# Second cross attention of an eight-layer kernel: another home for the query weight, other places for its splits, value products in alternating order

## The reference

```python
x = x + _L0_xattn_ref(_layernorm(x), ctx, ...)      # first cross attention
x = x + _L0_ffn_ref(_layernorm(x), ...)             # first feed-forward, 28 experts
x = x + _L1_xattn_ref(_layernorm(x), ctx, mask, Wq, Wk, Wv, Wo, q_norm_w, k_norm_w)
x = x + _L1_ffn_ref(_layernorm(x), ...)             # second feed-forward
...                                                 # four more layers

def _L1_xattn_ref(hidden_states, cross_attention_states, attention_mask, Wq, Wk, Wv, Wo, q_norm_w, k_norm_w):
    H, KVH, HD = (32, 8, 128)
    q = (hidden_states @ Wq.T)...   # 32 query heads of 128
    k = (cross_attention_states @ Wk.T)...   # 8 key heads
    v = (cross_attention_states @ Wv.T)...   # 8 value heads
    q = _rmsnorm(q, q_norm_w)
    k = _rmsnorm(jnp.repeat(k, GROUPS, axis=1), k_norm_w)
    scores = q @ k.T / sqrt(HD) + attention_mask
    probs = softmax(scores)
    return (probs @ v)... @ Wo.T
```

## Time and profile before

| | |
|---|---|
| time, median of 3 runs | 1603.42 us (1601.63 to 1606.4) |
| the profiled execution | 1602.04 us, its span 1600.3 us |
| TensorE busy | 1512.0 us, 94% of the span |
| VectorE busy | 1054.3 us, 66% |
| ScalarE busy | 815.2 us, 51% |
| GpSimd busy | 358.2 us, 22% |
| DMA | 60.23 MB, mean 38 GB/s |
| second cross attention, first to last query product | 690.3 to 1298.9 us of the span |

### The profile page before, as it was taken

How to read it: one execution, slowest core, us unless ns; L and a number is a source line. 1 busy time by engine, 2 the same in 40 slices (tenths; PEclk the granted TensorE clock), 3 DMA queues, 4 the chain that set the end, 5 groups by cost and what they waited for, 6 DMA issues and landing times.

```text
span 1600.3 us, 27791 instructions
## 1 busy us (share of the span) xinstructions
PE 1512.0 (94%) x9626; PEld 1324.2 (83%) x9626; DVE 1054.3 (66%) x2557; ACT 815.2 (51%) x2862; POOL 358.2 (22%) x370
## 2 busy tenths in 40 slices
PE   6999999999999999979999999999999998789996
PEld 5999999999999987868888888888888877667775
DVE  6566556655665568766666666666666677787775
ACT  4456455544554554345655555555555542454542
POOL 4102010210111021122313132222222221543420
PEclk9999999999999999989999999999999999898998
DMA  5100100100001000010101010101100001111001
GB/s 201 38 27 27 41 27 27 67 27 28 28 27 40 27 26 27 27 40 28 40 28 42 25 67 1 67 15 52 41 27 31 5 8 53 44 54 33 21 14 56
DMA packets 14193, 60.23 MB, mean 38 GB/s; under 512 B 2036, under 2 KB 3444, under 8 KB 8936
## 3 DMA queue, kind: packets, MB, share of 16 engines
q1 hardware_dynamic: 14056, 58.46, 10.2%
HBM read 56.36 MB, written 2.10 MB: 37 GB/s over the span
## 4 chain that ended last, share of the span: by engine, by line
PE 52%; issue 29%; DVE 11%; POOL 4%; ACT 3%; DMA 0%; POOLq 0%; DVEq 0%; SPq 0%; ACTq 0%
PE psY L843 12%; PE psQ L768 8%; PE psKV L788 8%; PE psSO L831 2%; PE psSO L737 2%; PE psQ L753 2%; PE psTP L753 1%; POOL wo L474 1%; PE psTP L798 1%; PE psSO L738 1%; PE psTP L816 1%; PE psQ L699 1%; PE psSO L712 1%; PE psKV L712 1%; PE psQ L1108 1%
## 5 line engine op out<-in xcount | busy, mean ns | idle before, releaser
L843 PE MATMUL psY<-wo,oT 128*128 128x512 f32 x1536 | 386.3, 400 | 1.8 <-DVE oT L1669 1.3
L843 PEld LDWEIGHTS psY<-wo,oT 128*128 128x128 f32 x1536 | 279.6, 189 | 66.3 <-POOL wo L474 2.2
L768 PE MATMUL psQ<-wq,hT 128*128 128x512 f32 x768 | 212.3, 414 | 0.1
L474 POOL TENSOR_TENSOR wo<-stage_o,wo 128x512 fp32r<-128x512 f32 (+2 forms) x71 | 91.7, 1320 | 322.3 <-ACT wo L1239 322.3
L575 POOL TENSOR_TENSOR rms<-ms_eps,minus_half 128x5 f32<-128x5 f32 x64 | 74.7, 1167 | 390.1 <-DVE ms_eps L1832 390.1
L768 PEld LDWEIGHTS psQ<-wq,hT 128*128 128x128 f32 x768 | 137.5, 192 | 25.0 <-DVE wq L1669 1.5
L1308 ACT ACTIVATE prob<-s_sb,neg_mx 128x64 f32<-128x64 f32 x256 | 86.1, 337 | 110.4 <-DVE neg_mx L1819 110.4
L1311 ACT ACTIVATE prob<-wide,neg_mx 128x128 f32<-128x128 f32 x256 | 99.7, 391 | 74.5 <-DVE neg_mx L1819 74.3
L1239 ACT ACTIVATE pT<-psTP 128x512 fp32r<-128x512 f32 (+1 forms) x128 | 62.3, 487 | 131.9 <-PE psTP L816 131.9
L788 PEld LDWEIGHTS psKV<-wkv,arena 128*128 128x128 f32 x768 | 99.6, 190 | 18.6 <-DVE kT L1669 14.3
L1669 DVE TENSOR_TENSOR pT<-psTP,pT 128x512 fp32r<-128x512 f32 (+1 forms) x128 | 70.6, 551 | 65.9 <-ACT pT L1239 65.1
(11 more groups left out here) (287 smaller groups left out, 3243.5 us busy)
## 6 DMA issues: line engine op xcount, KB each, us to landing
stage_q<-in_wq SPq DMA_DIRECT2D x16, 1024.0 KB, 5.2
stage_o<-in_wo SPq DMA_DIRECT2D x16, 1024.0 KB, 4.8
stage_kv<-in_wkv SPq DMA_DIRECT2D x12, 512.0 KB, 3.6
stage_q<-in_ctx SPq DMA_DIRECT2D x16, 256.0 KB, 2.8
stage_o<-in_ctxT SPq DMA_DIRECT2D x2, 1024.0 KB, 6.6
stage_q<-in_base SPq DMA_DIRECT2D x2, 1024.0 KB, 5.0
out<-x_res SPq DMA_DIRECT2D x8, 256.0 KB, 2.3
x_res<-in_x SPq DMA_DIRECT2D x1, 1536.0 KB, 12.4
```

The source lines that it names most:

```text
L474: g.tensor_tensor(dst[LO], stage, dst[HI].bitcast(f32), ALU.subtract).then_inc(ld[what + "_lo"], 1)
L768: m = mm(psQ[:], lat(xl, k, n), wq[:, wl, k, :], start=k == 0 and i == 0, stop=k == KT - 1 and i == 2)
L843: m = mm(psY[:], oT[:, ol, h, :], wo[:, wl, h, :], start=h == 0 and i == 0, stop=h == HQ - 1 and i == 2)
```

## The change

1. `attend` of the second attention goes over the passes outside and the batches inside, so its six products alternate between partitions 0 to 63 and 64 to 127.
2. The query weight gets two homes. Loads with an odd number from 9 on go to part 0 of `hT`, even ones to `wq` (`wq1_in_context`, `wq_slice`); the moving operand is there read in eight runs of 64 columns (`by_eight`). So the next group's weight is split while the present one is used: a quarter in each of steps 3, 4, 5 and 6 of a group (`high_wq1` on ScalarE, `low_wq1` on GpSimd). GpSimd now makes all four low parts, VectorE none.
3. In steps 2 to 7 of a group GpSimd waits for `prob` of the step before (the normalised probabilities) ahead of its weight splits, of the output, key and value weights too.
4. Load 9, the first group's, is split in the first feed-forward (steps 4 to 7 on ScalarE, after norms 2 to 5 on GpSimd), and the key and value weight before the last two norms.
5. `k_scale` is gone: `kT_hi` scales while it copies, and `kT_lo` is one instruction that scales and subtracts, both from the PSUM bank.
6. At the passage to the attention the first query product comes ahead of the transposes of the norm of tile 6, which move from the feed-forward into the first `kv_proj`.

```diff
@@ -358,6 +358,15 @@
         return psS[:, 2 * P:3 * P] if n < 4 else psP[:, 0:P]
+    def wq1_in_context(load):
+        return load >= 9 and load % 2 == 1
+    def wq_slice(load, hl, k):
+        return hT[:, hl, k, :, 0] if wq1_in_context(load) else wq[:, hl, k].rearrange("p (n t) -> p n t", n=NT)
+    def by_eight(ap):
+        return ap.rearrange("p (n t) -> p n t", n=NT)
@@ -468,10 +477,10 @@
-        def low(what, dst, stage, hi_count):
+        def low(what, dst, stage, hi_count, done=None):
...
             pool.wait_ge(ld[what + "_hi"], hi_count)
-            g.tensor_tensor(dst[LO], stage, dst[HI].bitcast(f32), ALU.subtract).then_inc(ld[what + "_lo"], 1)
+            g.tensor_tensor(dst[LO], stage, dst[HI].bitcast(f32), ALU.subtract).then_inc(ld[done or what + "_lo"], 1)
@@ -517,6 +526,10 @@
                 low("wo", halves(wo, k), stage_o[:, k], count + k + 1)
+        def low_wq1(load, k):
+            low("wq", (wq_slice(load, HI, k), wq_slice(load, LO, k)), by_eight(stage_q[:, k]), load * 4 + k + 1,
+                "wq_lo" if k < 2 else "wq_lo_v")
@@ -562,8 +575,9 @@
             ln_rstd(2, n)
-            if n == 6:
-                low_wq(9)
+            if 2 <= n < 6:
+                low_wq1(9, n - 2)
+            if n == 5:
@@ -574,8 +588,11 @@
                                 ALU.pow).then_inc(s["rms"], 1)
+            if t.exists and t.res(8) in (2, 3, 4, 5, 6, 7):
+                pool.wait_ge(s["prob"], t.back(1).c + 1)
+            if 3 <= t.res(8) < 7 and t.exists:
+                low_wq1(t.div(8) + 10, t.res(8) - 3)
             if t.res(8) == 7 and t.exists:
-                low_wq(t.div(8) + 10)
@@ -709,7 +726,8 @@
                 for i, (xl, wl) in enumerate(PASSES):
-                    m = mm(ring3(t)[:], lat(xl, k, t), wq[:, wl, k, :], start=k == 0 and i == 0, stop=False)
+                    m = mm(by_eight(ring3(t)[:]), lat(xl, k, t), wq_slice(WQ_DENSE[f.index], wl, k),
+                           start=k == 0 and i == 0, stop=False)
@@ -765,13 +783,15 @@
                     for i, (xl, wl) in enumerate(PASSES):
-                        m = mm(psQ[:], lat(xl, k, n), wq[:, wl, k, :],
+                        m = mm(by_eight(psQ[:]), lat(xl, k, n), wq_slice(st.div(NT) + a.wq0, wl, k),
...
                     pe.wait_ge(setup["ctxT"], 8)
+                    pe.wait_ge(FS["x_add"], NT)
+                    ln_transpose(2, NT - 2, lambda: pe.wait_ge(LNS[2]["lo"], ln_at(2, NT - 2)))
@@ -820,15 +840,17 @@
                 n = u.res(NT)
-                for b in range(2):
+                if a.index == 0:
+                    for b in range(2):
+                        for i, (vl, pl) in enumerate(PASSES):
+                            m = mm(psO0[:, b * 256:(b + 1) * 256], a.v[:, n, vl, b * HD:(b + 1) * HD],
+                                   pT[:, pl, b * 256:(b + 1) * 256], start=i == 0, stop=i == 2)
+                else:
                     for i, (vl, pl) in enumerate(PASSES):
-                        if a.index == 0:
-                            lhsT, rhs = a.v[:, n, vl, b * HD:(b + 1) * HD], pT[:, pl, b * 256:(b + 1) * 256]
-                        else:
+                        for b in range(2):
                             rows = slice(b * S, (b + 1) * S)
-                            lhsT, rhs = a.v[rows, u.res(a.ring), vl, 0:HD], pT[rows, pl, 0:256]
-                        out = psO0[:, b * 256:(b + 1) * 256] if a.index == 0 else psO[:, b, 0:256]
-                        m = mm(out, lhsT, rhs, start=i == 0, stop=i == 2)
+                            m = mm(psO[:, b, 0:256], a.v[rows, u.res(a.ring), vl, 0:HD], pT[rows, pl, 0:256],
+                                   start=i == 0, stop=i == 2)
@@ -952,7 +974,7 @@
                 hidden_transpose(f, u)
-            if 0 <= v < NT - (f.index == 0) and next_ln != 4:
+            if 0 <= v < NT - 2 * (f.index == 0) and next_ln != 4:
@@ -1251,6 +1273,9 @@
+        def high_wq1(load, k):
+            high("wq", wq_slice(load, HI, k), by_eight(stage_q[:, k]), (load + 1) * 16)
@@ -1286,11 +1311,13 @@
-                if a.rms:
-                    act.wait_ge(s["wq_used"], st.t * 4 + 4)
-                else:
-                    act.wait_ge(s["q_units"], st.t + 2)
-                high_wq(st.div(8) + (10 if a.rms else 1))
+                act.wait_ge(s["q_units"], st.t + 2)
+                high_wq(st.div(8) + 1)
+            def next_wq1(st):
+                need(act, s["wq_used"], st.div(8) * 32)
+                high_wq1(st.div(8) + 10, st.res(8) - 3)
@@ -1326,11 +1353,11 @@
                 act.wait_ge(s["k_tr"], a.kv_n(st) + 1)
-                src = k_sb[:, HD:2 * HD] if a.rms else psKV[:, 0:2 * keys]
                 if a.rms:
-                    act.wait_ge(s["k_scaled"], st.t + 1)
-                copy(a.kT[:, st.res(a.ring), HI], src).then_inc(s["kT_hi"], 1)
+                    nc.scalar.activation(a.kT[:, st.res(a.ring), HI], psKV[:, 0:HD], ACT.Identity,
+                                         scale=wqk[:, 2:3]).then_inc(s["kT_hi"], 1)
+                    return
+                copy(a.kT[:, st.res(a.ring), HI], psKV[:, 0:2 * keys]).then_inc(s["kT_hi"], 1)
@@ -1380,7 +1407,9 @@
                     unit_hi(k)
-                if t.exists and not early and t.res(8) == (7 if a.rms else 6):
+                if t.exists and a.rms and 3 <= t.res(8) < 7:
+                    next_wq1(t)
+                if t.exists and not a.rms and not early and t.res(8) == 6:
@@ -1463,11 +1492,12 @@
                      hT[:, hl, k, :, 0:4:3, :].bitcast(f32)).then_inc(setup["ctxT"], 1)
-            if t == 8:
+            if 4 <= t < 8:
+                act.wait_ge(setup["ctxT"], t + 1)
+                high_wq1(9, t - 4)
+            if t == 7:
...
                 high_wkv(5)
-                act.wait_ge(FS["dense"], NT)
-                high_wq(9)
@@ -1842,11 +1872,6 @@
-            def k_scale(st):
-                dve.wait_ge(s["k_tr"], a.kv_n(st) + 1)
-                V.tensor_scalar(k_sb[:, HD:2 * HD], psKV[:, 0:HD], wqk[:, 2:3], None, ALU.mult).then_inc(s["k_scaled"], 1)
@@ -1857,8 +1882,12 @@
                 dve.wait_ge(s["kT_hi"], a.kv_n(st) + 1)
-                src = k_sb[:, HD:2 * HD] if a.rms else psKV[:, 0:2 * keys]
-                sub_hi(a.kT[:, st.res(a.ring), LO], src, a.kT[:, st.res(a.ring), HI]).then_inc(s["kT_lo"], 1)
+                if a.rms:
+                    V.scalar_tensor_tensor(a.kT[:, st.res(a.ring), LO], psKV[:, 0:HD], wqk[:, 2:3],
+                                           a.kT[:, st.res(a.ring), HI].bitcast(f32), ALU.mult,
+                                           ALU.subtract).then_inc(s["kT_lo"], 1)
+                    return
+                sub_hi(a.kT[:, st.res(a.ring), LO], psKV[:, 0:2 * keys], a.kT[:, st.res(a.ring), HI]).then_inc(s["kT_lo"], 1)
@@ -1926,8 +1955,8 @@
                     qk_normalise(t)
-                if t.exists and t.res(8) == (7 if a.rms else 6):
-                    low_wq(t.div(8) + (10 if a.rms else 1))
+                if t.exists and not a.rms and t.res(8) == 6:
+                    low_wq(t.div(8) + 1)
@@ -1935,8 +1964,6 @@
                 if a.kv_new(t):
-                    if a.rms:
-                        k_scale(t)
@@ -2015,8 +2042,6 @@
                 ln_lo(f.ln, NT - 1)
-            if f.index == 0 and t == NT + 2:
-                low_wq(9)
```

## The result

The changed kernel takes 1586.44 us (median of 4 runs, 1586.05 to 1588.07) where the kernel before, beside it, took 1602.94: a ratio of 0.9896, 95% interval 0.9878 to 0.9913. That is 16.5 us, against 20.2 forecast as a difference and 1583 as a time. Timed again on another chip it took 1586.08 against 1604.54, a ratio of 0.9884 (0.9866 to 0.9901), 18.5 us. The profiled execution took 1586.25 us, its span 1584.4.

The account below looks back on a forecast made before the run. TensorE was taken as the bound, busy 579.99 of 593 us. The terms 9.9 + 4.2 + 4.1 + 2.0 = 20.2 us came off the profiled 1602.04, giving 1581.8, or 1583 us as a median; range 1576 to 1590, 8-in-10 range 1574 to 1595.

Parts of the forecast that it names:

- a group's step 0 above 9.8: Sign of being wrong: the first step of a group of eight still taking over 9.8 us, where it took 10.64.
- the waits for `kT`: Sign of being right: TensorE's weight loads wait under 2 us in all for `kT`, where they waited 14.3.
- The key product of step 0: Sign of being right at the passage from the feed-forward: this product starts at about 691 us instead of 695.29.
- Query weight in two homes: Steps 7 and 0 of each group: 1.42 us of excess goes, seven times, 9.9 us; ends 6.4 and 9.9.
- lower end of 6.4: Query weight's gain if half of the wait for `kT` stayed, 0.5 us in each group, 3.5 in all.
- I take the whole excess: Steps 7 and 0: all of 0.08 + 1.34 = 1.42 us over a plain step vanishes, seven times, 9.9 us.
- `k_scale`: Behind step 2, `kT`'s low part reads PSUM and ends earlier: 0.6 us, seven times, 4.2; ends 0 and 5.3.
- The passage: From feed-forward to attention: query product first, its weight split early; 4.1 us, with 2.2 below and 5.5 above.
- The end: Step 63: TensorE's waits of 1.27 for `prob` and 0.76 for `oT` both go, 2.0 us, between 0 and 3.
- Value products and strided weight: Reordering the six value products and reading the query weight in eight runs of 64 columns: 0 each.
- the rival of 15 us: Value products do gain, as the old order ran one after the other but for one pair: 15.4 us more, 1568; chance 0.06.
- The rival of half found again elsewhere: Stalls return in the feed-forward (4.4), step 7 (3.5) and step 2 (4.2), leaving 8.1 us: 1595; chance 0.17.

Follow-up runs that it names:

- x1: The kernel before with only the order of the value products changed, by pass and then by row half: 1605.49 us, 1.0007 of the kernel before.
- x4: The changed kernel with step 0's key and value products waiting for each half of their weight where read: 1579.55 us (0.9854), the second time 1583.57 (0.9874).
- x5: The changed kernel without GpSimd's waits for `prob` in steps 2 to 7: 1587.81 us, 0.9899 of the kernel before.
- x3: The changed kernel with VectorE's scaled key copy put back and both parts of `kT` made from it in SBUF: 1592.83 us, 0.9927 of the kernel before.
- x6: The changed kernel with the transposes of tile 6's norm back in the feed-forward, ahead of the first query product: 1588.52 us, 0.9901 of the kernel before.
- x9: The changed kernel with the scaled key copy and the old place of tile 6's transposes both put back: 1592.57 us, 0.9937 of the kernel before.

## Why the prediction was right, and where its terms were not

The bound, TensorE, the sign and the range were right. The time came out 3.4 us above the forecast. Of the signs that the prediction named, `neg_mx` (0.17 us throughout), the value products, the weight read in runs and `prob` came as said. But "a group's step 0 above 9.8", one of its signs of being wrong, came too, at 10.02, and the waits for `kT` are 2.4 us, not under 2. The key product of step 0 starts at 693.95, not at about 691, but TensorE stood 3.3 us later already when the feed-forward began. By its terms:

**Query weight in two homes: 9.9 forecast, 5.1 measured**, below even my lower end of 6.4: 0.06 in step 7 and 10.65 - 10.02 = 0.63 in step 0, seven times, and 0.2 more in one step 7 that took 9.59 before (9.60 in `x1`). The step that failed is "I take the whole excess". The prediction had GpSimd's 2.75 us for the key and value weight "beside it", because the list named only `kT`. That split was late too, by 0.14 us less, and became the wait. `x4` shows it, as taking that wait alone away brings step 0 to 9.30, 5.1 us in all. GpSimd's waits behind `prob` are worth about 2 us of the gain (`x5`).

**`k_scale`: 4.2 forecast, 6.75 measured by undoing it.** Behind step 2, 0.57 against 0.6: right, and for the reason given, as `x3` has the low part at 1.04 us and the changed kernel at 0.35. What I left out is steps 60 to 62, where the norm's transposes wait for the low part of `pT`, which stands behind `kT` on VectorE (1.05 us), 0.8 at the end, and 0.05 in each step 0.

**The passage: 4.1 forecast, 4.7 up to the key product.** The size is right by a wrong working. I put the 5.16 us of the first query product down to the clock; its last three products had to wait for VectorE's split, which ended at 694.44, and `x1` shows the waits, 0.85 and 0.73 us, at full clock. And 2.9 of the 4.7 come from splitting early (`x6`), not from the order. Up to the query transposes 4.5 are left, as 4.78 follow where 4.61 did: the 0.2 that I had put down. What follows to step 8 varies with the clock: 71.2 and 72.7 us in the two profiles of the changed kernel.

**The end: 2.0 forecast, 2.4 measured** (36.11 against 33.72 from step 63's start to the feed-forward's transposes, both without half clock). The profile of before has 37.33 there, with a stretch of half clock in it. `prob` went; `oT` keeps 0.71 of 0.76, so the working was off there too. Of the 2.4, 0.8 belong to `k_scale` (`x3`) and 1.6 to the query weight (`x9`).

**Value products and strided weight: 0, as forecast.** `x1` refutes the rival of 15 us. The Trainium skill's order rule ("TensorE: Matmul & The Clock Gate", The mechanism: products in program order, only weight loads pulled ahead) does not describe this pattern: three products of one row half and then three of the other take 0.63 us, alternating ones 0.62, one half alone 0.96. For the weight, the products from `hT` and from `wq` have the same mean in one window:

```profile
L786 PE MATMUL psQ<-wq,hT 128*128 128x512 f32 x372 | 100.7, 408 | 0.0
L786 PE MATMUL psQ<-hT 128*128 128x512 f32 x288 | 78.0, 408 | 0.0
```

**The rival of half found again elsewhere** had one of its three places right, the key and value split of step 7. It left 3.5 us there, and 0.72 x 7 = 5.0 stayed. In the feed-forward GpSimd's splits begin 0.2 us behind the start of `xn`, which takes 0.54 us all the same.

Together: 5.1 for the groups, 4.0 + 1.05 for `k_scale`, 4.7 for the passage and 2.4 for the end make 17.3 us. The two measurements gave 16.5 and 18.5. That the time came within 3.4 us of the forecast is in part luck: one term was 4.8 us too large, and the others together 1.9 too small, in part for reasons that the prediction didn't have.

## What to carry to other kernels

A wait has one name in the list, but several things can be late. Before counting a stall as gone, find when each of the other operands of the waiting instruction was ready: the second latest is what remains. Split a wait along the order in which its data are read, before moving work to make it shorter. Where a product is long and its clock low, read the rows of the weight loads as well, and look for the same place in a second profile: products stretched by half clock can fill a wait.

## What the runs showed of the hardware

- Where half clock falls differs between executions of one kernel, here by 3.1 us within 1420 to 1440 us, though the totals of four runs lie within 2.4 us (1584.33 to 1586.72).
- A VectorE instruction of 128 x 128 took 0.98 to 1.04 us with all operands in SBUF beside GpSimd's splits, and 0.35 with one of them in PSUM. One that started 0.2 us before GpSimd's split took its plain 0.54 us (`xn`), and the split 1.48 instead of 1.29.
- Six products over 64 rows overlap in pairs whether the program has them alternating or as three and three (0.62 and 0.63 us, against 0.96 when all six read one row half).
